# Layer 1's end in a graph network: GpSimd collects the self loops' factors ahead of the open segments' exchange

## The reference, cut to what matters

```
for r in range(8):
    mask = [edge_type == r, all self loops]
    h = x @ W[r];  e = leaky_relu(s[src] + d[dst]);  w = exp(e - max over dst)
    alpha = w / denom[dst]
    out += segment_sum(alpha * h[src], dst) + bias[r]
```

## Time and profile before

| | |
|---|---|
| median of 3 runs | 5696.48 us (5688.84 to 5698.95) |
| the profiled execution, its own time | 5697.31 us |
| its span | 5695.6 us |
| POOL busy | 3560.6 us, 63% |
| DVE busy | 4391.7 us, 77% |
| PE busy | 2580.8 us, 45% |

### The profile page before, as it was taken

One profiled execution on the slowest core, in us unless ns is written; L12 is line 12 of the kernel. 1 busy time (PEld: TensorE's weight loads), 2 busy tenths in 40 slices (PEclk: granted clock), 3 DMA queues, 4 the chain that ended last, 5 costly groups with the idle time before them and its releaser, 6 DMA issues.

```text
span 5695.6 us, 60196 instructions
## 1 busy us (share of the span) xinstructions
PE 2580.8 (45%) x8833; PEld 1211.4 (21%) x8833; DVE 4391.7 (77%) x11920; ACT 762.9 (13%) x1961; POOL 3560.6 (63%) x3631
## 2 busy tenths in 40 slices
PE   0000022047677710000555555555577777736993
PEld 0000012012256610000322122222233333312332
DVE  8899979159879999765577777774688878889992
ACT  0000000013200000454022222221000000002331
POOL 0777777720067788776577777772677777724651
PEclk9999999988779965555577878775799989968995
DMA  9000017134244433887255655651799999937980
GB/s 358 4 2 2 2 44 283 59 134 150 78 172 161 158 132 115 311 301 242 70 175 182 182 182 179 183 163 47 270 310 310 308 309 307 310 114 257 332 309 16
DMA packets 464764, 1028.64 MB, mean 181 GB/s; under 512 B 142937, under 2 KB 258063, under 8 KB 434724
## 3 DMA queue, kind: packets, MB, share of 16 engines
q1 hardware_dynamic: 160026, 509.52, 24.8%
q10 hardware_dynamic: 172682, 300.27, 14.7%
q0 software_dynamic: 131840, 216.96, 13.9%
HBM read 552.59 MB, written 470.64 MB: 180 GB/s over the span
## 4 chain that ended last, share of the span: by engine, by line
POOL 37%; issue 22%; DVE 17%; PE 14%; DMA 6%; DVEq 2%; ACT 1%; POOLq 0%; SPq 0%; ACTq 0%
POOL arena L622 22%; POOL weights L651 14%; PE psum L1148 4%; PE psum L1149 4%; DMA arena<-tab,ring 4%; PE psum L1199 3%; DVE arena L1495 2%; DVE arena L1504 2%; DVE arena L1470 1%; PE psum L982 1%; DVE arena L1957 1%; DVE arena L1786 1%; DVE arena L1698 1%; POOL agg L642 1%; DVE arena L1790 1%
## 5 line engine op out<-in xcount | busy, mean ns | idle before, releaser
L622 POOL DMA_INDIRECT arena<-tab,ring x2352 | 2341.9, 996 | 717.4 <-issue 700.6
L1148 PE MATMUL psum<-arena,ident 128*128 128x512 f32 x1176 | 760.5, 734 | 763.7 <-DMA arena<-tab,ring 518.5
L1470 DVE SCALAR_TENSOR_TENSOR arena<-arena,ns 128x64 f32<-128x64 f32 (+2 forms) x2351 | 869.5, 370 | 305.8 <-issue 121.6
L651 POOL DMA_INDIRECT weights<-ring x784 | 802.2, 1023 | 381.6 <-issue 381.6
L1149 PE MATMUL psum<-arena,ident 128*128 128x512 f32 x1176 | 713.1, 693 | 0.0
L1148 PEld LDWEIGHTS psum<-arena,ident 128*128 128x128 f32 x1176 | 254.3, 232 | 1180.1 <-issue 856.9
L968 PE MATMUL psum<-ident,hst 128*64 128x128 f32 x175 | 43.3, 409 | 878.1 <-DVE hst L1376 878.1
L1342 DVE SCALAR_TENSOR_TENSOR arena<-arena,base 128x280 f32<-128x280 f32 (+1 forms) x784 | 382.7, 488 | 52.3 <-issue 31.4
L716 POOL TENSOR_TENSOR arena<-arena,score 128x256 f32<-128x256 f32 x294 | 232.5, 815 | 280.8 <-DMA arena<-spill 127.1
L611 POOL DMA_INDIRECT put<-arena,zidx x75 | 74.0, 987 | 529.7 <-DVE arena L1548 399.3
L1199 PE MATMUL psum<-arena,ident 128*128 128x512 f32 x784 | 362.2, 608 | 68.9 <-DVE arena L1957 68.4
(11 more groups left out here) (344 smaller groups left out, 3949.9 us busy)
## 6 DMA issues: line engine op xcount, KB each, us to landing
put<-zero SPq DMA_DIRECT2D x98, 1040.0 KB
arena<-put SPq DMA_DIRECT2D x98, 1040.0 KB, 7.6
spill<-arena ACTq DMA_DIRECT2D x98, 1024.0 KB, 5.4
arena<-spill SPq DMA_DIRECT2D x98, 1024.0 KB, 7.7
state<-arena ACTq DMA_DIRECT2D x147, 512.0 KB
put<-zero ACTq DMA_DIRECT2D x14, 3584.0 KB
arena<-put SPq DMA_DIRECT2D x98, 512.0 KB, 3.7
weights<-zero SPq DMA_DIRECT2D x1, 44800.0 KB, 130.7
```

Source lines behind the costliest of these rows:

```text
L622: pool.indirect_dma_start(out=rows[:, h, k, :], out_offset=None, in_=table[:, :], in_offset=bass.IndirectOffsetOnAxis(ap=ring[:, h, word + ...
L651: pool.indirect_dma_start(out=weights0[:, :], out_offset=bass.IndirectOffsetOnAxis(ap=ring[:, u, k:k + 1], axis=0), in_=ringf[:, u, K + k: ...
L1148: pe.matmul(place, lhsT=ident[:, :], rhs=rows_of[0][:, s, columns, 0:width], start=True, stop=False)
L1470: beats.add(dve.scalar_tensor_tensor(out=rows[:, s, k, :], in0=before, scalar=mark(ns, g, k), in1=rows[:, s, k, :], op0=ALU.mult, op1=ALU. ...
```

## The change: the first collect moves ahead of the open segments

On POOL, the collect of the factors moves from behind `whole_segments` to directly behind the last gather of the edge part. Its `ready` waits for `weights_set` too. Then `whole_segments` follows, and then the collect of the sums with the wait that it had. No instruction is added or taken away except for the one further wait; the other engines' programs are the same.

```
             quads(pool, gather1)
+            ready((beta_out, 16), (weights_set, 1))
+            collect(1, betas, eidx, beta_n, before=0)
             whole_segments(1, state1, 1, open_sum[:, 0:D])
-            ready((beta_out, 16))
-            collect(1, betas, eidx, beta_n, before=0)
             ready((agg_in, 16 * NT))
             collect(1, state1, eidx, agg)
```

## The result

The changed kernel is slower: 5717.48 us median of 6 runs (5711.57 to 5720.23) against 5695.96 (5688.84 to 5698.95), a ratio of 1.0038 with a 95% interval of 1.0025 to 1.0051. That is 21.5 us more at the medians, 14 to 29 by the interval. The prediction said 5716.0, 19.5 us more, in a range of 5708 to 5724. The profiled execution took 5715.89 us, its span is 5714.1.

A forecast was written before the change was run, and what follows sets the result against it. Two chains were taken to end layer 1 within 0.5 us: POOL's sums, and DVE with PE. 22.18 us delay + 0.5 traffic - 2.74 - 0.42 coming back = 19.5 us longer, 5716.0 us, range 5708 to 5724.

The forecast's parts named there:

- The start: On POOL behind the edge part's last gather: waits already met, first gather of factors 0.30 us later, at 2671.66.
- Length and L631's delay: On POOL: 25 gathers, 37.33 us between first and last issue, then L631 at 2710.24 instead of 2688.06, 22.18 us late.
- The traffic's term: Early gathers on POOL land later amid the last groups' stores and loads: 0.5 us, bounds 0 and 4.4.
- What is queued behind: On DVE the node batches stand behind L1710's wait for the exchange, so they take the delay of 22.18 + 0.5 us.
- What comes back: First batch no longer waits for factors, 2.74 us back; L1737 no longer waits for POOL, 0.42 us back.
- The last groups of the edge part: Their stores and loads might be slowed by the early gathers, but 22 us of slack on DVE covers it.
- POOL's own chain: From L631 through the exchange, 9.93 us, to the sums' landing: would allow L1737 at 2752.78, 18.2 us gained, then waits for DVE.
- A: Rival at the end of the batches: POOL's chain decides, 18.2 us faster, 5678 us; chance 0.02.
- B: Rival in the node batches: PE is granted 2.4 GHz, 31.6 us saved, 12.1 us faster in all, 5684 us; chance 0.03.
- C: Rival in the batches: 8 us or more shorter beyond the 2.74, so cost 11 us or less, near 5706; chance 0.05.
- D: Rival on POOL's landings: traffic costs its upper bound, 4 us on top, 5720 us; upper part of the forecast's 0.90.
- The sum: Whole kernel: 22.18 + 0.5 - 2.74 - 0.42 = 19.5 us longer, 5716.0 us.

The follow-up runs named there:

- set 2: Second set of follow-up kernels, on a chip where the kernel before takes 5693 us; the changed kernel run again there: ratio 1.0040, +21.4 us.
- set 1: First set of follow-up kernels, each beside the kernel before on a chip where that one takes 7875 us; the changed kernel itself was not run there.
- the exchange behind batch 0: Changed kernel with DVE's wait for the open rows, addition and signal moved behind the first node batch: 5687.50 us, ratio to before 0.9991; in set 1 0.9992.
- the staging alone: Kernel before, with only DVE's exchange and bias sums moved behind the staging of two node batches: 5702.71 against 5702.52 us.
- the collect behind the stores: Changed kernel whose first gather of factors also waits for the last states' stores: ratio to before 1.0058, +33.5 us; in set 1 1.0031.

## Why the prediction was right

- **The start.** The first gather of factors 0.30 us behind the last of the edge part, both waits met: as said.
- **Length and L631's delay.** Said: 38.58 us from the first gather of factors to L631, plus 0.5 of traffic. Measured: 2710.17 - 2670.12 = 40.05, and 2712.28 - 2672.31 = 39.97 in set 2, 1.0 and 0.9 us more than the 39.08 of the sum.
- **The traffic's term was too small.** The first landing took 3.73 us instead of 2.21, the second 2.35: 1.5 us where I took 0.5, inside the bounds of 0 and 4.4. On the chip of set 1, in the kernel with the exchange behind batch 0, four waits for landings at a DMA share of 0.53 to 0.56 (3855 to 3900 us) took 3.39, 3.16, 2.62 and 2.70 us, against 2.06 to 2.20 in the kernel before at a share of 0.09; so gathers in traffic do land later. That traffic makes all of the 1.5 us here is not shown (last section). The 4.4 us that I worked out from the Trainium skill (DMA: Bandwidth & Descriptors, SWDGE vs HWDGE vs iDMA) as an estimate of equal shares did not come; the trace has a third of it.
- **What is queued behind.** Said: DVE idles some 26 us ahead of L1710. Measured 26.89 and 26.76. L1710 came 42.85 us behind the last gather's end instead of 19.12, 23.7 us later where the sum has 22.7. That this idleness is the loss is shown by moving the exchange on DVE alone, which gave 27 us back (24.5 in the traces).
- **What comes back.** Said: batches of 77 us instead of 80, L1737 with no wait for POOL. From L1710 to the last L1733's end it was 2789.86 - 2712.66 = 77.20 us, and L1737 waited for nothing. That is 2.85 us back where 2.74 were said.
- **The last groups of the edge part.** Said: slowed perhaps, and covered. Their carried sums stood 15.96 us behind the last gather's end instead of 15.63: 0.3 us, and DVE waited 26.89 us behind them.
- **POOL's own chain** was less than said: from L631 to the first gather of sums 6.70 us instead of 9.93. L633 followed DVE's signal by 0.9 us and not by 3, and landed in 2.3 and not in 3.3. It ended far ahead of DVE's chain, so this did not matter.
- **The rivals.** A, that POOL's chain decides, would have shown 18 us gained. B: the clock stayed at 0.50 in the batches. The Trainium skill (TensorE: Matmul & The Clock Gate, Part 1) would have it rise for a busy TensorE; here PE was busy for 61.19 of 78 us and it did not. C: the whole delay arrived. D did not come.
- **The sum.** 19.5 us said; 20.45 and 20.3 in the traces, 21.5 and 21.4 at the medians. By the first trace 23.73 - 2.85 - 0.43 = 20.45: the mechanism and every term are those of the sum, and what is missing is the 1.0 us of the traffic's term.

## What to carry to other kernels

A hole on one engine is worth filling only up to its length: 10 of 25 gathers fitted into some 17 us, and the other 15 went straight onto the first thing that another engine waits for. Before work is moved ahead of an exchange, look at what the partner has queued behind its half: here five batches stood behind a wait of 3.49 us that looked harmless. Look also at what an engine's work is really held by before moving it up: the staging alone gave nothing because the batches waited for factors, staging with ten early gathers gave 8 us, and with the first products early 15.

## What the runs showed of the hardware that was not expected

POOL paused once behind the end of the edge part, in every trace in which it had waited for another engine or for stores ahead of the first indirect DMA there. In before, L633 came 3.1 us behind DVE's addition, though POOL wakes in 0.8 us after a landing; the earlier trace rows has it as 2.95 us of "issue". It was the second indirect DMA behind the edge part. With the staging alone it was 3.1 again (2694.41 to 2697.48). In every kernel with gathers ahead of L631 it was 0.9. But with the collect behind the stores, the second gather had 1.69 us of "issue" instead of 0.30, and so it had on the chip of set 1, where POOL had waited 623 us; there 334 us of waiting ahead of L631 did not bring L633's pause back. So a long wait alone does not bring it. On that chip one batch has both the pause and a longer landing (1.70 us of "issue", then a wait of 3.39 us), so the two are different things. In the changed kernel no gather shows the pause; only the first landing is 1.5 us longer. In before, the profile has no DMA packet at all between 2690.8 and 2693.8, and with the collect behind the stores none of the queues that it calls "instruction" between 2689.9 and 2691.7, so a load of instructions by DMA does not show in the pause. Its cause is open; no run was made for it.
